# A fused adaLN, state and mixture-of-experts layer: the first two modulation weights loaded in halves

## What is computed

```
mod = (silu(c) @ wmod).reshape(1, 6, 1, 512)          # wmod is 512 x 3072
sa, ca, ga, sb, cb, gb = the six rows; ga and gb are kept away from zero
h = layernorm(x) * (1 + ca) + sa
x = x + ga * (tanh(h @ B.T) @ C.T + D * h)             # B is 256 x 512, C is 512 x 256
h = layernorm(x) * (1 + cb) + sb
x = x + gb * moe(h)                                    # 8 experts of width 352, top 2, and a shared expert
```

## Time and profile before

| | us |
|---|---|
| median of three runs | 546.07 |
| the three runs | 545.37 to 546.17 |
| the profiled execution, whole | 545.35 |
| its span, first to last instruction | 543.7 |

### The profile page before, as it was taken

How to read it: one execution, slowest core, us unless ns; L and a number is a source line. 1 busy time by engine, 2 the same in 40 slices (tenths; PEclk the granted TensorE clock), 3 DMA queues, 4 the chain that set the end, 5 groups by cost and what they waited for, 6 DMA issues and landing times.

```text
span 543.7 us, 11309 instructions
## 1 busy us (share of the span) xinstructions
PE 530.4 (98%) x3089; PEld 474.5 (87%) x3090; DVE 289.4 (53%) x607; ACT 196.0 (36%) x368; POOL 262.7 (48%) x221
## 2 busy tenths in 40 slices
PE   7999899999999999999999999999999999999996
PEld 3667788998999998899999999999999999998995
DVE  3789896686686667732222222222222222169887
ACT  1353725435434431333333333333333333212211
POOL 1499997667667366543025251036261600255540
PEclk9999999999999999999999999999999999999998
DMA  8999457543534388485654946254939412478862
GB/s 298 397 327 384 173 186 297 195 158 116 190 138 152 137 307 304 162 333 154 239 176 146 337 145 230 88 183 140 342 135 346 137 58 78 155 244 281 293 205 101
DMA packets 45386, 115.07 MB, mean 212 GB/s; under 512 B 4528, under 2 KB 4784, under 8 KB 45360
## 3 DMA queue, kind: packets, MB, share of 16 engines
q1 hardware_dynamic: 32560, 62.30, 32.8%
q0 software_dynamic: 12800, 52.43, 27.7%
HBM read 78.02 MB, written 36.70 MB: 211 GB/s over the span
## 4 chain that ended last, share of the span: by engine, by line
PE 81%; DVE 4%; issue 1%; ACT 1%; another core or an unknown queue 0%; DVEq 0%; ACTq 0%
PE bank L1043 15%; PE bank L1045 15%; PE bank L1044 15%; PE bank L1076 8%; PE bank L1074 8%; PE bank L1075 8%; PE bank L1081 4%; PE bank L1016 4%; PE bank L987 2%; PE bank L985 2%; PE bank L986 2%; DVE st L1713 1%; DVE gtl L1358 0%; DVE sel L1378 0%; ACT gth L809 0%
## 5 line engine op out<-in xcount | busy, mean ns | idle before, releaser
L590 POOL TENSOR_TENSOR wlo<-raw,whi 128x1408 f32 (+3 forms) x24 | 79.7, 3336 | 89.8 <-DMA whi<-w_all 80.2
L1043 PE MATMUL bank<-whi,thi 128*128 (+2 forms) x360 | 119.9, 333 | 0.4 <-DVE tlo L1524 0.4
L1045 PE MATMUL bank<-whi,tlo 128*128 (+2 forms) x360 | 116.4, 323 | 0.0
L1044 PE MATMUL bank<-wlo,thi 128*128 (+2 forms) x360 | 116.1, 323 | 0.0
L1806 DVE TENSOR_TENSOR gbuf<-s,bank 128x352 f32<-128x352 f32 x51 | 26.5, 519 | 106.2 <-PE bank L1045 103.1
L1074 PE MATMUL bank<-whi,gth 128*128 (+1 forms) x198 | 81.4, 411 | 0.0
L1075 PE MATMUL bank<-wlo,gth 128*128 (+1 forms) x198 | 78.0, 394 | 0.0
L1076 PE MATMUL bank<-whi,gtl 128*128 (+1 forms) x198 | 77.6, 392 | 0.0
L954 ACT ACTIVATE gth<-bank 128x384 fp32r<-128x384 f32 x50 | 24.7, 493 | 121.6 <-PE bank L1081 115.9
L1043 PEld LDWEIGHTS bank<-whi,thi 128*128 128x128 f32 x360 | 67.7, 188 | 0.7 <-issue 0.7
L1044 PEld LDWEIGHTS bank<-wlo,thi 128*128 128x128 f32 x360 | 67.8, 188 | 0.0
(11 more groups left out here) (225 smaller groups left out, 1000.5 us busy)
## 6 DMA issues: line engine op xcount, KB each, us to landing
raw<-w_all POOLq DMA_DIRECT2D x8, 2176.0 KB
whi<-w_all POOLq DMA_DIRECT2D x16, 704.0 KB, 11.3
h<-xs_rows SPq DMA_DIRECT2D x35, 256.0 KB, 2.8
ys_rows<-tmpa SPq DMA_DIRECT2D x35, 256.0 KB, 2.0
x_all<-wmod SPq DMA_DIRECT2D x6, 1024.0 KB, 9.7
whi<-w_all POOLq DMA_DIRECT2D x8, 768.0 KB, 5.3
hs_rows<-h SPq DMA_DIRECT2D x8, 512.0 KB, 5.0
mods<-hs_rows SPq DMA_DIRECT2D x7, 512.0 KB
```

Of the source, the lines that this page charges most:

```text
L590: pool.tensor_tensor(wlo[:, bass.ds(off + (SH + a), b - a)], raw[:, a:b], whi[:, bass.ds(off + (SH + a), b - a)].bitcast(F32), ALU.subtrac ...
L1043: pe.matmul(dst, xh[:, j, a], wh, start=(m == 0), stop=False)
L1044: pe.matmul(dst, xh[:, j, a], wl, start=False, stop=False)
L1045: mm = pe.matmul(dst, xl[:, j, a], wh, start=False, stop=(m == KD - 1))
```

## The change

`piece(0)` and `piece(1)` are issued as two transfers each, chunks 0 and 1 and then chunks 2 and 3, of 512 KB each. The first of them raises a new semaphore `l_half[i]`, the second the old one. `modulation(0)` and `modulation(1)` wait for `l_half[i]` ahead of chunk 0, and for the old semaphore ahead of chunk 2. SP issues two transfers more. All else is as it was.

```
+        l_half = [sem(f"l_half{i}") for i in range(2)]
...
-                sp.dma_start(ring[SLOT[i]], wm_v[WM[i]]).then_inc(l_wm[SLOT[i]], 16)
+                if i < 2:
+                    h = KD // 2
+                    sp.dma_start(ring[SLOT[i]][:, 0:h, :], wm_v[WM[i]][:, 0:h, :]).then_inc(l_half[i], 16)
+                    sp.dma_start(ring[SLOT[i]][:, h:KD, :], wm_v[WM[i]][:, h:KD, :]).then_inc(l_wm[SLOT[i]], 16)
+                else:
+                    sp.dma_start(ring[SLOT[i]], wm_v[WM[i]]).then_inc(l_wm[SLOT[i]], 16)
...
-                pe.wait_ge(l_wm[SLOT[i]], LOADED[i])
+                pe.wait_ge(l_half[i] if i < 2 else l_wm[SLOT[i]], 16 if i < 2 else LOADED[i])
                 for k in range(KD):
+                    if i < 2 and k == KD // 2:
+                        pe.wait_ge(l_wm[SLOT[i]], LOADED[i])
```

## The result

| | kernel before | changed kernel |
|---|---|---|
| median, 12 runs each | 545.54 us | 546.62 us |
| lowest and highest | 544.81 to 546.35 | 545.63 to 547.82 |
| profiled execution, and its span | 545.35, 543.7 | 545.63, 544.0 |

The ratio is 1.0016, with a 95% interval of 1.0009 to 1.0024: the change makes the kernel 0.9 us slower (0.5 to 1.3). PE starts earlier, and the kernel ends later.

What follows compares the result with a forecast made beforehand. PE's stream, busy 98% of the span, plus its stalls bounds the kernel. Modulations 0 and 1: 1.31 gained, all lost to piece 2; `clo` 0; `wlo` +1.1: 547.2 on the median 546.07; own range 546.6 to 547.7, whole 545.6 to 548.0.

Steps and rivals of the forecast that it cites:

- the turn lost to the long addition: DVE's `wlo`, held behind POOL's long addition L705, ends at 34.24; `h2` and the time come 1.1 us later; chance 0.50.
- Halves and landings: At PE's start, piece 1's first half lands 1.31 us ahead, at 10.72, and modulation 1 ends 1.31 us earlier.
- the wait in the middle: Modulation 1's wait for its second half, landing at 12.03, costs nothing: two chunks keep PE busy until 12.44.
- Piece 2 swallows it: After `turn_columns` PE waits 1.2 us for piece 2; modulation 2 starts at 17.28 to 17.4, gain at most 0.09.
- two more queue ends: In the load queue, two more transfers might add 0.12 us at 0.06 each; taken with the gain as 0.
- The rival of a fixed cost of each transfer: Load queue: two fixed costs in series bring piece 2 at 20.7, 3.4 us slower, 549.5; chance 0.03.
- SP's issues: Two more issues on SP move piece 2's issue from 4.78 to 5.7; the queue covers this by 9 us.
- The turns: DVE and POOL alternate at SBUF; `blo` ends at 20.51, `clo` stays at 30.5, POOL comes one instruction ahead.
- slower, more: Rival: POOL's lead is 0.7 to 1.0 instead of 1.3, adding up to 0.65 to +1.1: 547.7; chance 0.10.
- would get back the 1.25 of L1494: Case of the no-change rival (546.0, chance 0.27): `h2` loses 1.1 but regains 1.25 because DVE precedes POOL's L598.

Runs made afterwards that it cites:

- the second time: The unaltered changed kernel measured once more against the kernel before: 547.34 us against 545.76, ratio 1.0026 (1.0017 to 1.0036).
- the addition in two: Changed kernel with GpSimd's long addition as two instructions of 512 elements instead of one of 1024: 545.79 us against 545.78, ratio 1.0004.
- without the early start: Changed kernel's half transfers, but each modulation waits for both halves before it begins: 545.66 us against 545.78, ratio 1.0006 (0.9997 to 1.0015).
- the run with the turn given back: Changed kernel in which GpSimd's long addition into x also waits for the shared expert's first `wlo`: 546.31 us against 545.78, ratio 1.0014.
- the reversed turn in the kernel before: Kernel before, loads unchanged, with VectorE's first `wlo` made to wait for GpSimd's long addition: 548.13 us against 545.78, ratio 1.0043, 5 runs.
- piece 2 first with the addition in two: Changed kernel with piece 2 issued ahead of B and GpSimd's long addition as two instructions: 546.45 us against 545.76, ratio 1.0012.
- only piece 0: Changed kernel with only piece 0 in halves and piece 1 whole: 546.31 us against 545.68, ratio 1.0015 (1.0006 to 1.0024).
- GpSimd held: Changed kernel in which GpSimd's second step also waits for VectorE's sign of modulation 2: 546.26 us against 545.68, ratio 1.0012.
- the control: The kernel before measured once more against itself: 545.96 us against 545.76, ratio 1.0002 (0.9993 to 1.0011).

## Why the prediction was right

It said 547.2, +1.1 us, with the turn lost to the long addition; measured was +0.9 (0.5 to 1.3), 546.62, and +1.4 (0.9 to 2.0) the second time. That 547.2 is 0.6 too high lies in its starting point: three runs of the kernel before had a median of 546.07, twelve have 545.54. Step by step:

1. **Halves and landings**: piece 1's first half at 10.72 predicted, 10.6 measured; the wait in the middle free, as said. Piece 0's first half landed at 5.7 and not at 6.6, which changed nothing, since the zero matmuls held PE until 6.69.
2. **Piece 2 swallows it**: 17.28 to 17.4 predicted, 17.35; PE's wait 1.2 predicted, 1.38. The 0.12 that two more queue ends might have cost did not show clearly: from piece 0's landing to piece 2's it was 9.37, 9.40 and 9.38 with whole pieces, and with both pieces in halves 9.34 to 9.46 in five executions and 9.79 in a sixth (the addition in two); with one piece in halves 9.85 and 9.60. The rival of a fixed cost of each transfer, 3.4 us in all, is out: without the early start the same transfers gave a ratio of at most 1.0015.
3. **SP's issues**: piece 2 was issued at 6.02, not at 5.7, and the queue covered it.
4. **The turns**: `blo` 20.51 predicted, 20.43 measured; `guard`'s end 23.65 and 23.55; the addition's end 32.76 and 32.69; `wlo`'s end 34.24 and 34.17; the transposes 44.3 to 44.4 and 44.30. With less lead the turns moved as the rival "slower, more" has it: in the run with the turn given back the lead was 0.94, and `clo` ended 0.39 later after modulation 2's start. The divided addition and the reversed turn in the kernel before show the cause by taking it away and by putting it in.

What it got wrong is in the rivals. I wrote that DVE, coming 0.05 earlier than L598, would get back the 1.25 of L1494. Two executions came that way (the turn given back, and piece 2 first with the addition in two: `wlo` 0.18, `h2` 2.36), and nothing was got back: `h2` was held by the same product instead. Held work is not saved by going first if the next instruction needs the same turn; both executions lost another 0.6 us at the `wlo` after that. And I took start and landing times from one execution; between executions modulation 2's start moved by over a microsecond (16.61 to 18.22) and the end with it, which makes a forecast of turns from one trace a forecast of the likeliest order.

**What stays open.** Four variants without the lost turn in their profiles (no early start, only piece 0, GpSimd held, addition in two) have ratios of 1.0006, 1.0015, 1.0012 and 1.0004, a mean of 0.09%, while the control has 0.02%, each with about 0.09% either way. About 0.4 us may thus belong to the halves themselves, or to executions whose order of turns no profile caught. The first would leave the turn some 0.7 us of the mean loss of 1.15 us (0.16% and 0.26%), not all, and the closeness of +0.9 to the forecast of +1.1 would be in part luck. For the second speaks that one execution of each was profiled, and often one of the fastest: without the early start six runs took 545.28 to 545.66, the profiled one among them, and five took 546.41 to 546.90, with none between. An order like that of the run with the turn given back costs 0.3 us ahead of the `h2` transposes and 0.6 behind them, which is about that distance. That is an argument and not shown: no run here separates the two.

## What to carry to other kernels

Splitting a load so that its consumer starts early is worth only as much as the next load's landing lets through: follow the consumer to its second and third wait before counting the gain. What the early part does set free are the other engines, and if two of them take turns at SBUF, as VectorE and GpSimd did here, a shift of a microsecond reorders their turns. A long instruction that comes to stand ahead of one on the critical path costs its whole remaining length. Cutting it in two gave this back in one order of loads; in the other, a different instruction held the turn. Judge such changes by many executions, and by distances inside a trace rather than by its end.

## What the runs showed of the hardware

Times of the loads vary from execution to execution more than the effect sought: piece 2 landed between 16.61 and 18.12 us in the eleven executions with the same order of loads (issue plus time to land). The zero matmuls' loads change from a spacing of 0.85 to 0.43 us at a time that differs as well (by 5.1 us in the first profile of the kernel before, not before 6.8 in the run with the turn given back). The profile gives a granted clock of 1.00 for 1.5 to 6 us in each of the five executions read for it, so it does not show this change. Where PE waited for data after it this was covered, in the changed kernel too (modulation 1 waited until 10.64 for its first half). In the run with the turn given back it was not: the half landed at 10.7 and modulation 1 began at 10.86, behind modulation 0.

VectorE and GpSimd took turns in every meeting read here between instructions that read two tensors from SBUF, and small differences in time set the order: at 40.5 to 41.7 the product at 40.56 came ahead of the router's `wlo` at 40.61 in the first profile of the kernel before, and with the turn given back the `wlo` at 40.53 ahead of a product at 41.14.
